# Filter loads cut to their band, weights moved to the first stage, other loads moved and split in the middle stage of an audio tower kernel

## The reference, cut to what matters

```
fir_long = causal_dwconv(vf, fir_long_w.reshape(NH * DV, FIR_L))     # 63 taps, 256 channels, 384 positions
A = jnp.tril(jnp.einsum('bhnid,bhnjd->bhnij', kbc, kc), -1)
T = jnp.linalg.inv(jnp.eye(chunk) + A)                               # one 32 x 32 system per chunk
u = T @ vc
w = T @ kbc
```

## Time and profile before

| | us |
|---|---|
| median of 3 runs | 2713.1 (2710.72 to 2714.3) |
| the profiled execution | 2711.45 |
| its span, first to last instruction | 2709.7 |
| middle stage, from the first filter load to the third stage's first event | 764.45 to 932.48 |

### The profile page before, as it was taken

How to read it: one execution, slowest core, us unless ns; L and a number is a source line. 1 busy time by engine, 2 the same in 40 slices (tenths; PEclk the granted TensorE clock), 3 DMA queues, 4 the chain that set the end, 5 groups by cost and what they waited for, 6 DMA issues and landing times.

```text
span 2709.7 us, 53423 instructions
## 1 busy us (share of the span) xinstructions
PE 2412.4 (89%) x21052; PEld 1817.1 (67%) x21052; DVE 1929.9 (71%) x5233; ACT 1377.0 (51%) x2633; POOL 537.6 (20%) x373
## 2 busy tenths in 40 slices
PE   4888888888889689999999999999999999999997
PEld 3666666666568566677767777776777677777764
DVE  3888898998859246667767776777676667656655
ACT  3777777777734224444454444445444544454442
POOL 0333333333310001111111111111111111111111
PEclk9998999999987568999999999999999999999999
DMA  2666666666679702223212221322132223212200
GB/s 79 194 206 204 202 202 207 205 219 206 199 281 345 259 19 90 69 68 112 68 62 102 102 68 62 103 77 68 66 111 89 68 71 109 68 62 92 85 18 18
DMA packets 223162, 334.47 MB, mean 123 GB/s; under 512 B 113857, under 2 KB 190625, under 8 KB 213697
## 3 DMA queue, kind: packets, MB, share of 16 engines
q1 hardware_dynamic: 219744, 309.03, 34.3%
q10 hardware_dynamic: 2304, 12.58, 1.2%
q0 software_dynamic: 864, 9.44, 0.9%
HBM read 191.68 MB, written 164.23 MB: 131 GB/s over the span
## 4 chain that ended last, share of the span: by engine, by line
PE 40%; DVE 16%; ACT 6%; issue 3%; POOL 0%; DVEq 0%
PE bank L1543 6%; PE bank L1474 5%; PE bank L1533 5%; PE bank L1366 4%; PE bank L1485 3%; DVE DL L1875 3%; PE bank L1504 3%; ACT L1680 3%; DVE v_all L1961 3%; PE bank L1478 2%; PE bank L1397 2%; PE bank L1405 2%; PE bank L1452 1%; DVE e L1920 1%; ACT HE L1680 1%
## 5 line engine op out<-in xcount | busy, mean ns | idle before, releaser
L704 DVE SCALAR_TENSOR_TENSOR Y<-bank,convw,Y 128x383 f32<-128x383 f32 (+2 forms) x576 | 314.4, 605 | 7.0 <-ACT Y L580 7.0
L1543 PE MATMUL bank<-w2e,HE 128*128 128x256 f32 x1152 | 289.9, 388 | 12.1 <-DVE v_all L1961 9.2
L1961 DVE SCALAR_TENSOR_TENSOR v_all<-bank,we,v_all 128x256 f32<-128x256 f32 x576 | 242.7, 476 | 79.2 <-PE bank L1543 76.9
L432 PE MATMUL bank<-pb,wqkv 128*128 128x384 f32 x768 | 284.9, 501 | 10.6 <-issue 10.5
L1533 PE MATMUL bank<-v_all,w1e 128*128 128x384 f32 x768 | 285.8, 495 | 1.4 <-ACT HE L1680 1.4
L1841 DVE TENSOR_TENSOR L<-bank,b2g 128x48 f32<-128x48 f32 x32 | 6.6, 208 | 343.7 <-PE bank L1485 343.7
L1543 PEld LDWEIGHTS bank<-w2e,HE 128*128 128x128 f32 x1152 | 208.0, 192 | 49.5 <-issue 16.6
L1474 PE MATMUL bank<-v_all,w1g 128*128 128x384 f32 x512 | 201.8, 517 | 0.4 <-ACT v_all L1672 0.4
L1680 ACT ACTIVATE HE<-bank 128x384 f32<-128x384 f32 x192 | 94.3, 491 | 194.6 <-PE bank L1533 193.8
L432 PEld LDWEIGHTS bank<-pb,wqkv 128*128 128x128 f32 x768 | 137.4, 196 | 83.0 <-issue 24.6
L804 POOL TENSOR_TENSOR RR<-RS,minus_half 128x24 f32<-128x24 f32 x32 | 133.3, 4165 | 267.9 <-DVE RS L753 267.9
(11 more groups left out here) (211 smaller groups left out, 5342.2 us busy)
## 6 DMA issues: line engine op xcount, KB each, us to landing
packa<-pa SPq DMA_DIRECT2D x32, 1932.0 KB, 8.1
v_all<-packa SPq DMA_DIRECT2D x32, 1932.0 KB, 7.8
packb<-pb SPq DMA_DIRECT2D x32, 768.0 KB, 5.9
v_all<-packb SPq DMA_DIRECT2D x32, 768.0 KB, 6.9
toeplitz<-taps SPq DMA_DIRECT2D x128, 190.0 KB, 4.9
toep<-toeplitz SPq DMA_DIRECT2D x32, 760.0 KB, 9.4
packb<-fsk SPq DMA_DIRECT2D x32, 384.0 KB, 2.3
first_stage<-fl SPq DMA_DIRECT2D x32, 384.0 KB, 5.5
```

Source lines behind the costliest of these rows:

```text
L432: mm = pe.matmul(proj_bank[j][:, 0:T], wqkv[:, a, j * P:(j + 1) * P], xnT[:, a, :], start=(a == 0), stop=(a == HALF - 1))
L704: dve.scalar_tensor_tensor(out=Y[:, j, lag:T], in0=proj_bank[j][:, 0:T - lag], scalar=convw[:, j, CK - 1 - lag:CK - lag], in1=Y[:, j, lag: ...
L1543: mm = pe.matmul(expert_bank(b), HE[k % 2][:, b * P:(b + 1) * P], w2e[:, k, :], start=True, stop=True)
L1961: dve.scalar_tensor_tensor(out=HA[s][:, b, :], in0=expert_bank(b), scalar=we[s][:, b, k:k + 1], in1=HA[s][:, b, :], op0=ALU.mult, op1=ALU. ...
```

## The change

Six edits, all but the first two inside the middle stage.

1. `toeplitz` becomes [128, 256, 128]: of each row only 128 columns are stored, from column 0 for the rows 0 to 63 and from column 62 for the rows 64 to 127. The other 62 are zeros in either half.
2. `w1g` and `w1e` are loaded in the first stage, one DMA for each of the sequences 0 to 6 (`load_early`), into buffers that exist from the start. An unused semaphore of POOL (`v_kept`) goes.
3. A filter load is now two DMAs of 64 partitions. Each partition's piece of 8 x 128 numbers goes into rows of 128 at a pitch of 190, so that the pieces that land together shrink from 6080 bytes to 512. The columns 0 to 61 of the partitions 64 to 127 are never loaded: DVE clears them once per buffer ahead of the first solve, and PE waits for this behind `dense(5)`. The narrow product reads only the partitions 64 to 127.
4. `dense(3)` ahead of groups 8, 16 and 24 goes.
5. The packs are loaded behind all 32 filter loads, and the remaining weights come earlier: `w2e` at group 13.
6. A set of systems is loaded in three DMAs of 512 KB. Those of sets 1 and 2 start at steps 13, 23, 33, 43 and 53 of set 0, the last third of set 2 at step 21 of set 1 and behind the store of set 0, those of set 3 at steps 9, 17 and 25 of set 2.

```diff
-                        sp.dma_start(dram["toeplitz"][p], dram["taps"][:, bass.ds(P - 1 - p, TW)]).then_inc(expanded, 16)
+                        sp.dma_start(dram["toeplitz"][p], dram["taps"][:, bass.ds(P - 1 - p + (p // DH) * (FL - 1), P)]).then_inc(expanded, 16)
+                def load_early(c):
+                    if c == 0:
+                        sp.dma_start(early["w1g"][:, :, :], w["mlp_w1"][0:D].rearrange("(a p) n -> p a n", a=HALF))\
+                            .then_inc(early["early_loaded"], 16)
+                    elif c <= NE:
+                        sp.dma_start(early["w1e"][:, :, c - 1, :], w["ffn_w1"][c - 1].rearrange("(a p) n -> p a n", a=HALF))\
+                            .then_inc(early["early_loaded"], 16)
...
-                    sp.dma_start(toep[it % NT][:, :, :], dram["toeplitz"][:, it * CG:(it + 1) * CG, :])\
-                        .then_inc(toep_loaded[it % NT].sem, 16)
+                    for half in range(2):
+                        rows = slice(half * DH, (half + 1) * DH)
+                        sp.dma_start(toep[it % NT][rows, :, half * (FL - 1):half * (FL - 1) + P],
+                                     dram["toeplitz"][rows, it * CG:(it + 1) * CG, :]).then_inc(toep_loaded[it % NT].sem, 16)
...
-                    if it == groups - 6:
-                        load_packs(sp)
+                load_packs(sp)
                 load_factors(sp, setup_act)
...
                 dense(5)
+                pe.wait_ge(setup, CONSTANTS)
...
-                        if it and it % GI == 0:
-                            dense(3)
...
-                                mm = pe.matmul(acc[0:TW - P, o + NB:o + BLK * NB], toep[s][:, ch, P:],
-                                               v_all[:, it * CG + ch, 0:(BLK - 1) * NB],
+                                mm = pe.matmul(acc[0:TW - P, o + NB:o + BLK * NB], toep[s][DH:P, ch, P:],
+                                               v_all[DH:P, it * CG + ch, 0:(BLK - 1) * NB],
...
-                load(0)
-                pool.wait_ge(solve["step"], 21)
-                load(1)
+                for part in range(SG):
+                    load(0, part)
+                load(1, 0, 13)
+                load(1, 1, 23)
+                load(1, 2, 33)
+                load(2, 0, 43)
+                load(2, 1, 53)
                 store(0)
-                load(2)
+                load(2, 2, SOLVE_STEPS + 21)
                 store(1)
-                load(3)
+                load(3, 0, 2 * SOLVE_STEPS + 9)
+                load(3, 1, 2 * SOLVE_STEPS + 17)
+                load(3, 2, 2 * SOLVE_STEPS + 25)
...
+                for s in range(NT):
+                    dve.memset(toep[s][DH:P, :, 0:FL - 1], 0.0).then_inc(setup, 1)
```

More of the change, by code:

```diff
@@ L101, in audio_tower @@
             "taps": nc.dram_tensor("taps", [D, 512], F32, kind="Internal").ap(),
-            "toeplitz": nc.dram_tensor("toeplitz", [P, D, TW], F32, kind="Internal").ap(),
+            "toeplitz": nc.dram_tensor("toeplitz", [P, D, P], F32, kind="Internal").ap(),
         }
@@ L115, in audio_tower @@
         v_all = sb("v_all", [P, D, BLK * NB])
-        first_phase(nc, x, w, shared, v_all)
-        third_phase(nc, w, out, shared, third_phase_weights(nc, ctx), v_all)
+        early = early_weights(nc, ctx)
+        first_phase(nc, x, w, shared, v_all, early)
+        third_phase(nc, w, out, shared, third_phase_weights(nc, ctx, early), v_all)
 def make_constants(nc, ctx, ident, upper):
@@ L145, in _, with first_phase @@
                 sp.sem_inc(g.sem, g.per * g.primed)
-def first_phase(nc, x, w, shared, v_all):
+def first_phase(nc, x, w, shared, v_all, early):
     NB, dram, bank, ident, upper, expanded = (shared[k] for k in ("NB", "dram", "bank", "ident", "upper", "expanded"))
@@ L260, in first_phase @@
         at_copied = signal("at_copied", 2)
-        v_kept = signal("v_kept")
         prime(nc, signals)
@@ L354, in body @@
                         expand(c)
+                        load_early(c)
                     if b is not None:
@@ L371, in _ @@
                 body(c=NB - 1, s=1)
+                sp.wait_ge(early["early_loaded"], 16 * (1 + NE))
                 for s in range(2):
@@ L814, in body @@
                         for b in range(BLK):
-                            keep = pool.tensor_copy(v_all[:, :, c + b * NB], toks(pa[s], VTOK)[:, b, :])
-                        keep.then_inc(v_kept.sem, 1)
+                            pool.tensor_copy(v_all[:, :, c + b * NB], toks(pa[s], VTOK)[:, b, :])
                     if a is not None:
@@ L826, in _, with early_weights, third_phase_weights, sb @@
                 body(c=NB - 1, s=1)
-def third_phase_weights(nc, ctx):
+def early_weights(nc, ctx):
     def sb(name, shape):
         return ctx.enter_context(nc.sbuf_tensor(name, shape, F32))
-    w1g = sb("w1g", [P, HALF, MLP])
+    return dict(w1g=sb("w1g", [P, HALF, MLP]), w1e=sb("w1e", [P, HALF, NE, DE]),
+                early_loaded=ctx.enter_context(nc.semaphore("early_loaded")))
+def third_phase_weights(nc, ctx, early):
+    def sb(name, shape):
+        return ctx.enter_context(nc.sbuf_tensor(name, shape, F32))
+    w1g, w1e = early["w1g"], early["w1e"]
     w1s = sb("w1s", [P, MLP])
@@ L842, in third_phase_weights @@
     rclip = sb("rclip", [P, 1])
-    w1e = sb("w1e", [P, HALF, NE, DE])
     w2e = sb("w2e", [P, NE, D])
@@ L866, in load_third_phase_weight @@
     if n == 3:
-        load(tail["w1g"][:, :, :], w["mlp_w1"][0:D].rearrange("(a p) n -> p a n", a=HALF))
-    if n == 4:
         load(tail["w1s"][0:GATE_S, :], w["mlp_w1"][D:])
         load(tail["w2g"][:, :, :], w["mlp_w2"].rearrange("(m p) n -> p m n", m=MC))
-    if n == 5:
+    if n == 4:
         load(tail["b2g"][:, :], w["mlp_b2"].partition_broadcast(P))
         load(tail["anchors"][:, :, :].rearrange("p e d -> p (e d)"), w["ffn_anchors"].rearrange("e d -> (e d)").partition_broadcast(P))
-    if n == 6:
+    if n == 5:
         with nc.allow_non_contiguous_dma(reason="a few columns, once"):
             load(tail["b1g"][:, :], w["mlp_b1"].rearrange("(m p) -> p m", m=MC))
-    if n in (7, 8):
+    if n in (6, 7):
         with nc.allow_non_contiguous_dma(reason="a few columns, once"):
-            load(tail["router"][:, n - 7, :], w["ffn_proj_w"][:, (n - 7) * P:(n - 6) * P].rearrange("e p -> p e"))
-    if 9 <= n < 9 + NE:
-        load(tail["w1e"][:, :, n - 9, :], w["ffn_w1"][n - 9].rearrange("(a p) n -> p a n", a=HALF))
-    if n == 9 + NE:
+            load(tail["router"][:, n - 6, :], w["ffn_proj_w"][:, (n - 6) * P:(n - 5) * P].rearrange("e p -> p e"))
+    if n == 8:
         load(tail["w2e"][:, :, :], w["ffn_w2"].rearrange("e p n -> p e n"))
-WEIGHT_LOADS = 18
+WEIGHT_LOADS = 11
 CLEARED = 3 + 7
-CONSTANTS = 2 + NE - 1
+CONSTANTS = 2 + NE - 1 + 4
 def second_phase(nc, w, shared, v_all, stage, tail, solve, load_packs, load_factors):
@@ L909, in second_phase @@
         GI = DH // CG
-        toep_loaded = [signal(f"toep_loaded{s}", 16) for s in range(NT)]
+        toep_loaded = [signal(f"toep_loaded{s}", 32) for s in range(NT)]
         fl_ready = signal("fl_ready", 2, primed=2)
@@ L1026, in _, with load @@
                 X = solve["X"]
-                def load(g):
-                    pool.dma_start(X[g][:, :, :, :], systems[g]).then_inc(solve["loaded"][g % 3], 16)
+                def load(g, part, after=0):
+                    if after:
+                        pool.wait_ge(solve["step"], after)
+                    pool.dma_start(X[g][:, part, :, :], systems[g][:, part, :, :]).then_inc(solve["loaded"][g % 3], 16)
                 def store(g):
@@ L1224, in solve_begin @@
         def solve_begin(dve, g):
-            dve.wait_ge(solve_loaded[g % 3], 16 * (g // 3 + 1))
+            dve.wait_ge(solve_loaded[g % 3], 16 * SG * (g // 3 + 1))
             dve.memset(X[g][:, :, :, :].rearrange("p s j i -> p s (j i)")[:, :, ::SC + 1], 1.0).then_inc(solve_step, 1)
```

## The result

| | before | after |
|---|---|---|
| median, us | 2711.91 (2708.77 to 2714.3, 4 runs) | 2752.24 (2749.5 to 2754.11, 4 runs) |
| ratio after / before | | 1.0147, 95% interval 1.0131 to 1.0163 |
| profiled execution, span | 2711.45, 2709.7 | 2749.5, 2747.8 |
| middle stage | 764.45 to 932.48 | 767.99 to 970.86 |
| mean granted clock | 0.95 | 0.927 |

The account below looks back on a forecast made before the run. PE was taken to bound the middle stage: 877.1 + 16 x 2.68 + 2 of waits + 5.3 of tail = 927.3 against 932.48, so -5.2 us from 2711.45, giving 2706. The range was 2670 to 2718.

Parts of the forecast that it names:

- what bounds the stage: Middle stage: PE's filtering until 927.2 ends it, then ACT's tail; a group takes 3.30 us, or 5.98 at half clock.
- The 10.02 us wait: PE's wait before 897.18, from SP standing in front of the packs; it goes once the packs are loaded last.
- the narrow products: PE's filter products losing half their rows: change taken as 0, bounds 0 and -3 us.
- a fall near group 16: Filter: one late load near group 16, then half clock to the end; 2706 us, chance 0.46.
- the price of the filter load: Middle stage: a cut load of 524 kB was taken at 1.7 us, between 1.26 and 1.87.
- sum to be made at group 17: Group 17's load, due at 827.6: 22.4 us of transfers end at 829.0, so it comes 1.4 us late.
- the rule that the prediction weighed: Filter loads: line rate from 512 bytes, so pieces cost nothing and group 17's load lands at 826.8, in time.
- The third rival: SP's queue cannot feed the filter: preparation near 3.30 us, clock lost at groups 4 to 13; 2728, chance 0.19.
- The harmless wait: PE's filter: a wait of 0.65 us does not cost the clock, one of 2.97 us did.
- the rival: The clock holds in the filter and DVE ends the stage at 893.0; 2672 us, from 2668 to 2680, chance 0.35.
- the thirds: Set 0 in three loads: DVE +1 us, from -3 to +4, so DVE would end at 892.6.
- The first stage: Seven more loads and expansions a third smaller: change taken as 0, within 1 us either way.

Follow-up runs that it names:

- one_load_short: Kernel before with each filter load as one DMA of 128 partitions, taking only the first 128 columns in 512-byte pieces; 2711.15 us, ratio 1.0.
- run 6: Kernel before with each filter load issued as two DMAs of 64 partitions, rows whole; 2739.34 us, ratio 1.0104; its kernel is `two_loads_whole`.
- run 8: Kernel before with each filter load as two DMAs over all 128 partitions, four channels each; 2711.54 us, ratio 0.999; its kernel is `two_loads_channels`.
- two_loads_whole: Kernel before with each filter load issued as two DMAs of 64 partitions, rows whole (pieces of 6080 bytes); 2739.34 us, ratio 1.0104.
- two_loads_channels: Kernel before with each filter load as two DMAs over all 128 partitions, four channels each (pieces of 3040 bytes); 2711.54 us, ratio 0.999.
- wide_loads: Kernel after with whole filter loads again (edits 1 and 3 undone), the rest kept; 2694.93 us, ratio 0.9947 against before.
- run 10: Kernel before without the three identity products (`dense(3)`) ahead of groups 8, 16 and 24; 2700.16 us, ratio 0.9963.
- run 11: Kernel before with edits 2, 5 and 6 alone; 2689.56 us, ratio 0.9917; its kernel is `wide_dense`.
- wide_dense: Kernel after with whole filter loads (edits 1 and 3 undone) and identity products ahead of groups 8, 16 and 24 back; 2689.56 us, ratio 0.9917 against before.
- bands_two_queues: Kernel after with each filter load's half for partitions 64 to 127 issued by ACT instead of SP; 2745.52 us, ratio 1.0114 against before.

## Why the prediction was wrong

**Right: what bounds the stage.** PE ends it, its groups take 3.30 and 5.98 us, ACT's tail is 5.25, and the filter at half clock never speeds up by itself (185 us of it here). The 10.02 us wait went with the packs, the narrow products cost the same (0.66 against 0.67 per eight records), the clears hid under `dense(5)` (done at 770.6, the filter began at 775.39), the third stage kept its length, and one wait cost the clock to the end. All that stood in the forecast; it gives 2706 with a fall near group 16. (For a fall at group 0 it gives 877.1 + 32 x 2.68 + 2 + 5.3 = 970.2 and 2749; the 2747 of the prediction is 2 us under its own formula.) What came is a fall at group 1: by the same formula 877.1 + 31 x 2.68 + 1.75 + 5.3 = 967.2, 34.7 behind 932.48; the stage grew by 34.8.

**The step that failed: the price of the filter load.** I took 1.7 us between 1.26 and 1.87. On the scale on which the old load is 1.87 (415 GB/s), the table's 3.22 against 2.15 makes the new one 2.8, outside my bounds. I had looked at one of its two properties. The pieces I weighed, and their dear end held: "1.87 again if they eat the whole gain" is what `one_load_short` shows (2.04 against 2.15). That each DMA now writes 64 partitions I counted only as two more issues to prepare. Runs 6 and 8 show what it costs: 3.39 against 2.12 us per group at equal bytes and equal number. With 3.2 us per group there is no sum to be made at group 17: beside sets, stores and weights the loads can't keep up with PE's 3.30 from the first quarter on, and at the stage's start, with set 0 beside them, they fail at group 0 or 1 in every kernel that has the halves and doesn't cover that wait.

On the pieces, `one_load_short` speaks against the rule that the prediction weighed (the Trainium skill, "DMA: Bandwidth & Descriptors", opening table: line rate from 512 bytes): 258 GB/s at full share against 363. On the halves there is a rule that I had not weighed, and it was the one against this change. The Trainium skill, "SBUF — State Buffer", "Door 1: The DMA port swizzle", says that a DMA's bandwidth depends on how many of the 16 ports its partitions reach, and by its table partitions 0 to 63 reach eight of them; half of its 436 GB/s would be 218, an estimate from that page. `two_loads_whole` moved 230 at full share, 5% above it, so the trace agrees roughly with its size. That ports are the cause no run here shows; they show the dependence on the half.

**The third rival came true in time, not in its mechanism.** It put the end "from group 0 on" at 2747 and gave the whole case 0.19, by the thought that preparing the DMAs may need near 3.30 us. An issue did become dearer (a pair 1.26 us from 792 on, against 0.33 for the one before), but this is far from 3.30, in `two_loads_channels` a pair takes 0.80 us, and in after the engines were full while the loads were late, not idle behind SP: the preparation was not it. Its evidence against, "the first quarter has 0.86 of the engines busy with the larger loads", was the misleading row: 0.86 busy leaves room only if the new load is no dearer than the old.

**The harmless wait.** I took 0.65 us as harmless and 2.97 as fatal. The runs fill the gap: 1.70 and 1.75 us took the clock, 1.66 and 1.81 (`wide_loads`) didn't. So for waits of about 1.7 to 1.8 us these runs leave it open; every wait seen in the filter from 1.91 us on took it. That the times of `wide_loads` lie in two groups fits that, but only one of its executions has a trace.

**The gain was there.** Edits 2, 4, 5 and 6 with whole loads gave -18 us in the median (edit 4 alone gave -11 in run 10, edits 2, 5 and 6 alone -24 in run 11), and with the clock held -27 (2686), where the rival had 2672. DVE ended at 901, not at 892.6: the stage began 5.0 us later in this execution (769.49), and DVE waited 15.86 us for the thirds of set 0 instead of 11.16, 4.7 more where I had bounded the thirds at +4. The thirds cost this only beside whole filter loads: in after DVE has set 0 10.6 us after the stage's start, before it was 11.5.

**The first stage** grew by 3.5 us, beyond my 1. Over the kernels the middle stage starts anywhere from 764.3 to 772.2, at 764.3 in `wide_dense`, which has the early weights, and at 772.2 in `one_load_short`, whose first stage is that of before. So the early weights need not cost anything; what moves the start from one execution to the next I haven't found.

## What to carry to other kernels

Before a load is cut to fewer bytes, write down both what a piece is and which partitions each DMA writes: here the pieces ate the saving, and halves of 64 partitions made each byte half as dear again. If a load has to be split, split it so that each DMA still covers all 128 partitions: `two_loads_channels` did so at no cost. Where one late load costs the clock for all that is left, the price of a load has to be known at the start of the stage, where all first loads come together, and products that only give the clock back are worth keeping as long as waits like the 1.70 and 1.75 us here are left. Change the order and size of loads one at a time: 18 us of gain lay under 57 of loss.

## What I had not expected of the hardware

- Two DMAs of 64 partitions each move 230 GB/s at full share, two over 128 partitions with the same bytes 367.
- Two halves that are under way at once, from two queues, move 290 GB/s together, as one DMA over 128 partitions with the same pieces does; one at a time they move 199 (`bands_two_queues`).
- Pieces of 512 bytes move 258 GB/s at full share, pieces of 3040 and of 6080 bytes 367 and 363.
- A wait of 1.70 us was enough for the clock to fall, and 1.81 us in another kernel was not.
- With three queues full at once, half of the first eight filter loads landed after more than 12.4 us (`bands_two_queues`); with all eight in one queue the median was 10.2 (after, from 768 to 778).
